# Attention values in four column groups and channel-major projections in a vision tower

## The chip, the cores and the metric

The kernel runs on one core of one Trainium2 chip. All data are float32. The metric is the device time of one launch in microseconds, as the median of the runs shown below. One further execution was taken by the hardware profiler, and all rows below are from it.

## What is computed

64 images of 3 x 224 x 224 pass through a small tower. Each is cut into 196 patches of 16 x 16; a patch becomes a token of 256 channels. Then, with h as the tokens and LN a layer norm without weights:

```python
h  = patches @ W.T + b                                   # tokens, 196 x 256
# selective scan (state space layer), inner width 512, 16 states
xb, z = split(h @ in_proj.T);  xb = silu(causal_conv4(xb))
dt_in, B, C = split(xb @ x_proj.T);  dt = softplus(dt_in * dt_w + dt_b)
state = scan(exp(dt * A) * state + (xb * dt) * B);  y = sum_n(state * C) + xb * D
h  = LN(h + (LN(y) * g + b) * silu(z) @ out_w.T)
# channel mix: token mixed with the token before it
r  = sigmoid(xr @ W_r);  k = square(relu(xk @ W_k));  h = LN(h + r * (k @ W_v))
# attention, 8 heads, queries and keys 4 wide, values 32 wide
s  = leaky_relu(q @ k.T / 2);  h = LN(h + gamma * softmax(s) @ v)
# eight experts, top 2 by the gate
h  = LN(h + sum_e(gate_e * (h @ We_e.T + be_e)))
```

## The kernel before, in words

The program is one software pipeline over images. An image needs 16 groups of scan work (`GROUPS`: four blocks of 128 inner channels times four groups of four states), and the pipeline's time is counted in slots, 16 per image. Each constant `AT_...` is the slot of a step relative to the first scan group of its own image; so at any time the scan of one image lies beside steps of images ahead of it (patches, embedding, convolution at negative slots) and behind it (output, feed-forward, attention, experts at slots up to 90). Every engine has a function `step` that walks through the 16 slots and, within a slot, through its steps in the order in which they are written; engines execute in that order and wait for each other by semaphores. Slots are not synchronised across engines: an engine runs ahead until a semaphore stops it.

**Scan.** In each slot GpSimd (POOL) forms X = u * B for one group (`inputs`, L472, 128 x 784), VectorE (DVE) scans it in two halves (`scan_group`, L1089), POOL multiplies by C (`times_c`, L482), and TensorE (PE) sums the states by transposing matmuls with the identity into YB (`sum_states`, L599). ScalarE (ACT) makes the decay exp(dt * A) into PSUM (`decay`, L892) ahead of each scan half and drains the sums (`drain_y`, L899). X has a ring of six buffers, the decay one of two. u = dt * x is one POOL operation per image (L462).

**PSUM.** Three one-bank tiles G0, G1, G2 and one two-bank tile SB are shared by all other steps. `G0_USES` and its sisters say which steps use which bank, in order of slots; a step waits until the use before it is drained.

**Output.** After the layer norm of y, `turn_y` brings it to channels on partitions, ACT applies gain and bias into y3 (L907), POOL multiplies by silu(z) (L525). `project_out` has tokens on the output's partitions: per block of 98 tokens four products of 256 columns (L620), and the residual hT is added by accumulating transposes (L623).

**Channel mix.** h1 is turned back to channels (`h1T`). r and v are token-major products of 256 columns (`token_major`, L639), k is channel-major (`mix_keys`, L647). ACT drains k with a ReLU (L939), POOL squares it (L515), ACT takes the tanh of r (L934); DVE forms (1 + tanh) * v and adds h1 (L1122, L1125), both token-major.

**Attention.** Queries and keys are two products of 96 output rows each (L656), masked by ACT so that the heads can share a contraction. A unit is four heads of one block of 98 queries; an image has four. Per unit: scores (L668, two row groups of 32 partitions, 392 columns), leaky ReLU (L956), row maximum (DVE, L1136), four exponentials (L963), eight transposes (L678), a PSUM drain (L971), and the values: eight products with the probabilities as the 98 x 98 stationary operand and 33 moving columns (L691), the 33rd being ones, so that the row sum comes out as well. DVE divides and adds the residual (`attended`, L1148 to L1153).

**Loads.** SyncE (SP) issues all DMAs in its own `step` order: pixels in 16 pieces, the projections dt, B, C stored to DRAM and spread back over 128 partitions (L401, L407), the gates likewise (L413, L419), and the output.

`keep_busy` (L546) issues matmuls whose result is used by nobody, at the slots `AT_WARM`, as often as `WARM` says. A float32 matmul of the program appears in the trace as two MATMUL records with their LDWEIGHTS, a transpose as one.

Of the kernel before, what the change touches and what calls it, by code (L numbers as in the profile page):

```python
# [7 lines left out]
ALU = mybir.AluOpType  # L8
# [3 lines left out]
P = 128  # L12
# [6 lines left out]
BLK = 2  # L19
# [22 lines left out]
QKP = 3 * QK  # L42
# [23 lines left out]
AT_TAP = -22  # L66
# [3 lines left out]
AT_XD = -12  # L70
AT_XPROJ = -12
AT_XPROJ_OUT = -12
AT_PROJ_STORE = -12
AT_DT_LOAD = -9
# [10 lines left out]
AT_Y_STATS = 18  # L85
AT_Y_STD = 20
AT_Y_NORM = 21
AT_TURN_Y = 22
AT_YG = 23
AT_Y3 = 25  # L90
AT_OUT = 26
AT_OUT_STATS = 27
# [8 lines left out]
AT_V = 34  # L101
AT_FFN = 35
AT_FFN_STATS = 35
AT_FFN_STD = 38
AT_FFN_NORM = 39
AT_H2T = 41
AT_H2T_OUT = 42
AT_QK = 42
AT_QK_OUT = 43
AT_VALUES = 47  # L110
AT_VALUES_OUT = 48
AT_SCORES = (43, 45, 46, 49,)
# [12 lines left out]
AT_GATE = 68
AT_GATE_IN = 69
AT_GATE_EXP = 70
AT_TOP2 = 70
AT_WS = 70
AT_WS_OUT = 71  # L130
AT_GATE_STORE = 70
AT_GATE_LOAD = 71
AT_H3T2 = 75
AT_SCALE = (75, 75, 76, 77,)
AT_PAIR = (76, 77, 78, 78,)
AT_ACC_OUT = 80
AT_MOE_T = 86
AT_MOE_STATS = 88
AT_MOE_STD = 89
AT_MOE_NORM = 89  # L140
# [54 lines left out]
def vit_tower(nc, x, w_tok, b_tok, w_in, conv_w, conv_b, w_xproj, a_log, d_par, dt_w, dt_b, w_out, ln_g, ln_b,  # L195
              w_r, w_k, w_v, mu_r, mu_k, w_qk, b_q, b_k, w_vv, b_v, gamma, w_g, b_g, w_e, b_e,
              ident, q_mask, k_mask, rank_of, proj, gates, out):
    with ExitStack() as ctx:
# [32 lines left out]
        bk = sb("bk", [QKP, 1])  # L231
        bqm = sb("bqm", [QKP, 2])
        bkm = sb("bkm", [QKP, HU // 2])
# [9 lines left out]
        kmask = sb("kmask", [QKP, HU // 2])  # L243
# [27 lines left out]
        rs = sb("rs", [TB, BLK, D])  # L271
# [6 lines left out]
        vs = [sb(f"vs{i}", [TB, BLK, HEADS, DV + 1]) for i in range(2)]  # L278
# [3 lines left out]
        rg = sb("rg", [TB, HU])  # L282
# [63 lines left out]
        normed = {n: sem(f"normed_{n}") for n in LN}  # L346
        y3_ready = sem("y3_ready")
        before_step = sem("before_step")
# [5 lines left out]
        av_step = sem("av_step")  # L354
        gate_step = sem("gate_step")
# [13 lines left out]
        CONSTS = 16  # L369
# [10 lines left out]
        def _(sp):  # L380
# [40 lines left out]
            def step(b, par):  # L421
                for g in range(GROUPS):
                    def at(slot):
                        return live(b, par, g, slot)

                    for ng in range(GC):
# [4 lines left out]
                    for s, q in at(AT_GATE_STORE):  # L431
                        store_gates(s)
                    for s, q in at(AT_DT_LOAD):
                        after(sp, dt_ready, s)
                        spread_rows(s, dtin[:].rearrange("p (o t) -> p o t", o=1), 0, 1, dtin_landed)
                    for s, q in at(AT_LOAD):
                        load(s)
                    for ng in range(GC):
                        n0 = NG * ng
                        for s, q in at(AT_B[ng]):  # L440
# [925 lines left out]
```

## Time and profile before

| what | us |
|---|---|
| median of 3 runs (lowest to highest) | 4683.52 (4680.42 to 4685.36) |
| the profiled execution's own time | 4687.52 |
| its span | 4685.5 |
| PE busy | 4386.0 (94%) |
| POOL busy | 4332.2 (92%) |
| DVE busy | 3726.6 (80%) |
| ACT busy | 3705.0 (79%) |

The span runs from the first to the last instruction of the profiled execution. Busy is the time in which an engine executed something, over the whole span; the pipeline's fill at the start and its drain at the end are included, so the steady part is denser. Overlapping instructions of one engine are counted once.

### The profile page before, as it was taken

The numbers are of one execution on the slowest core, as the hardware profiler recorded it, in microseconds if no ns is written. First come the engines' busy times: TensorE is split into PE (matmuls) and PEld (weight loads), VectorE is DVE, ScalarE is ACT, GpSimd is POOL, SyncE is SP. The second block draws the span as 40 slices with busy tenths as digits, with TensorE's granted clock in tenths as the row PEclk, the third lists the DMA queues.
The fourth block names the chain that finished last, engine by engine and source line by source line (L and its number), as shares of the span: only waits on it lengthen the run. The fifth ranks groups of instructions, "written<-read, shape, count | busy, mean of one in ns | idle before, by whom it ended". The sixth has DMA issues, their size and how long they took to land.

```text
span 4685.5 us, 92000 instructions
## 1 busy us (share of the span) xinstructions
PE 4386.0 (94%) x31744; PEld 3882.0 (83%) x31744; DVE 3726.6 (80%) x7504; ACT 3705.0 (79%) x8898; POOL 4332.2 (92%) x3272
## 2 busy tenths in 40 slices
PE   4689999999999999999999999999999999999998
PEld 3578888888888888888888888888888888888777
DVE  3578888888888888888888888888888888888753
ACT  4688888888888888888888888888888888888752
POOL 4999999999999999999999999999999999999950
PEclk8799999999999999999999999999999999999987
DMA  4223233223223223223323323323322322322200
GB/s 101 64 68 77 61 76 86 58 71 86 60 74 81 62 76 78 67 70 78 72 67 76 75 64 76 84 58 73 86 59 71 85 61 75 80 65 72 68 18 28
DMA packets 730607, 328.77 MB, mean 70 GB/s; under 512 B 631542, under 2 KB 655392, under 8 KB 729888
## 3 DMA queue, kind: packets, MB, share of 16 engines
q1 hardware_dynamic: 730144, 322.89, 27.9%
q8 instruction: 254, 4.16, 0.4%
q14 instruction: 209, 1.71, 0.1%
HBM read 307.88 MB, written 14.90 MB: 69 GB/s over the span
## 4 chain that ended last, share of the span: by engine, by line
PE 33%; ACT 29%; DVE 23%; issue 7%; POOL 5%; DMA 1%; SPq 1%; ACTq 0%; DVEq 0%; POOLq 0%
PE G L719 15%; DVE X L1089 9%; ACT dA L892 8%; PE YB L599 5%; DVE xbs L1066 4%; PE SB L576 4%; PE SB L668 3%; ACT pT L971 3%; PE G L639 3%; POOL X L482 2%; POOL X L472 2%; ACT y L907 2%; ACT xbs L849 2%; ACT dt L880 2%; ACT ysb L926 2%
## 5 line engine op out<-in xcount | busy, mean ns | idle before, releaser
L1089 DVE TENSOR_TENSOR_SCAN X<-dA,X 128x392 f32<-128x392 f32 x2048 | 1873.3, 957 | 370.2 <-ACT dA L892 327.1
L482 POOL TENSOR_TENSOR X<-X,Cb 128x784 f32<-128x784 f32 x1024 | 1896.9, 1852 | 24.9 <-DVE X L1089 24.6
L472 POOL TENSOR_TENSOR X<-u,Bb 128x784 f32<-128x784 f32 x1024 | 1898.9, 1854 | 7.0 <-DMA Bb<-proj_rows 6.8
L892 ACT ACTIVATE dA<-dt,negA 128x195 f32<-128x195 f32 x4096 | 1519.4, 418 | 144.5 <-DVE X L1089 122.0
L599 PE MATMUL YB<-idn,X 128*98 128x128 f32 x8192 | 1074.5, 276 | 40.1 <-POOL X L482 40.0
L599 PEld LDWEIGHTS YB<-idn,X 128*98 128x98 f32 x8192 | 912.1, 129 | 96.1 <-POOL X L482 50.9
L719 PE MATMUL G<-hg,we 128*128 128x196 f32 x4096 | 723.5, 333 | 7.4 <-DVE hg L1205 7.4
L719 PEld LDWEIGHTS G<-hg,we 128*128 128x128 f32 x4096 | 680.5, 192 | 46.5 <-issue 45.0
L576 PE MATMUL SB<-hT,win 128*128 128x196 f32 x2048 | 373.6, 335 | 34.8 <-ACT hT L840 34.4
L691 PEld LDWEIGHTS G<-vs,pT 98*98 98x98 f32 x4096 | 401.4, 172 | 3.8 <-ACT pT L971 2.4
L691 PE MATMUL G<-vs,pT 98*98 98x33 f32 x4096 | 395.7, 252 | 1.9 <-ACT pT L971 1.9
L576 PEld LDWEIGHTS SB<-hT,win 128*128 128x128 f32 x2048 | 335.3, 190 | 69.8 <-ACT hT L840 50.0
L963 ACT ACTIVATE pr<-pr,nmx 98x196 f32<-98x196 f32 x1024 | 378.3, 450 | 12.9 <-DVE nmx L1136 12.6
L1066 DVE SCALAR_TENSOR_TENSOR xbs<-SB,cw,xbs 128x195 f32<-128x195 f32 (+2 forms) x768 | 267.1, 412 | 94.6 <-ACT xbs L849 90.5
L899 ACT ACTIVATE ysb<-YB 98x256 f32<-98x256 f32 x256 | 97.6, 381 | 250.3 <-PE YB L599 250.3
L956 ACT ACTIVATE pr<-SB 98x784 f32<-98x784 f32 x256 | 209.1, 817 | 93.9 <-PE SB L668 89.9
L567 PE MATMUL G<-patT,wtok 128*128 128x196 f32 x1536 | 272.8, 335 | 1.5 <-ACT patT L831 1.5
L668 PE MATMUL SB<-km,qm 32*98 32x392 f32 x1024 | 233.6, 530 | 36.1 <-DVE xbs L1074 35.1
L567 PEld LDWEIGHTS G<-patT,wtok 128*128 128x128 f32 x1536 | 260.3, 195 | 2.0 <-issue 1.9
L1205 DVE TENSOR_TENSOR hg<-G,Gb 128x784 f32<-128x784 f32 x256 | 241.1, 963 | 21.4 <-PE G L719 18.7
L1136 DVE TENSOR_REDUCE nmx<-pr 98x4 f32<-98x784 f32 x256 | 243.1, 950 | 16.2 <-ACT pr L956 6.6
L620 PE MATMUL G<-wout,y 128*98 128x256 f32 x1024 | 250.9, 389 | 0.0
(145 smaller groups left out, 6621.8 us busy)
## 6 DMA issues: line engine op xcount, KB each, us to landing
Bb<-proj_rows SPq DMA_DIRECT2D x256, 392.0 KB, 4.3
Cb<-proj_rows SPq DMA_DIRECT2D x256, 392.0 KB, 4.9
Gb<-gate_rows SPq DMA_DIRECT2D x64, 784.0 KB, 4.5
px<-in_x SPq DMA_DIRECT2D x1024, 36.8 KB
out<-ob SPq DMA_DIRECT2D x64, 196.0 KB
dtin<-proj_rows SPq DMA_DIRECT2D x64, 98.0 KB, 3.1
we<-in_w_e SPq DMA_DIRECT2D x1, 2048.0 KB
proj_rows<-pj SPq DMA_DIRECT2D x64, 25.3 KB
```

The costliest lines, as they stand in the source:

```text
L472: tt(X[(GROUPS * s + g) % RING][:], u[q % 2][:, c:c + 1, :].broadcast_to([P, NG, T]), Bb[:, NG * ng:NG * (ng + 1), :], ALU.mult).then_inc( ...
L482: tt(t[:], t[:], Cb[:, n0:n0 + NG, :], ALU.mult).then_inc(prod_ready, 1)
L567: last = mm(o[:, m * T:(m + 1) * T], lhsT=wtok[:, k, m * P:(m + 1) * P], rhs=patT[:, half * COLORS + c, :], start=(k == 0), stop=(k == KP ...
L576: last = mm(o[:, j // 2, (j % 2) * T:(j % 2 + 1) * T], lhsT=win[:, k, m * P:(m + 1) * P], rhs=src[:, k, :], start=(k == 0), stop=(k == DC ...
L599: last = mm(YB[0:TB, k * P:(k + 1) * P], lhsT=X[(GROUPS * s + g) % RING][:, j, k * TB:(k + 1) * TB], rhs=idn[:], is_transpose=True, start= ...
L668: last = mm(o[0:TB, j, :], lhsT=qm[mine, n % 2, k * TB:(k + 1) * TB], rhs=km[mine, :, :].rearrange("p h t -> p (h t)"), start=True, stop=True)
L691: last = mm(o[0:TB, j * (DV + 1):(j + 1) * (DV + 1)], lhsT=pT[:, j // 2, at:at + TB], rhs=vs[q % 2][:, k, h0 + j, :], start=(k == 0), stop ...
L719: last = mm(o[:, m * T:(m + 1) * T], lhsT=we[:, k, at:at + P], rhs=hg[p % GRING][:, e, k, :], start=(p == 0 and e == 0 and k == 0 and m == 0),
L892: last = go(dA[i % DRING][:, j, 1:T], dt_[q % 2][:, c, 1:T], ACT.Exp, scale=negA[:, c, n:n + 1])
L963: last = go(pr[i % PRING][:, j, :], pr[i % PRING][:, j, :], ACT.Exp, bias=nmx[i % PRING][:, j:j + 1])
L1066: last = v.scalar_tensor_tensor(out=xbs[:, c, k:], in0=S.tile[:, c // 2, at:at + T - k], scalar=cw[:, c, TAPS - 1 - k:TAPS - k], in1=xbs[: ...
L1089: v.tensor_tensor_scan(t, dA[i % DRING].rearrange("p n t -> p (n t)"), t, 0.0, ALU.mult, ALU.add).then_inc(scan_done, 1)
```

## The change

- The values have the value heads as stationary operand (98 x 32) and the probabilities as moving one (98 columns). The four heads of a unit write to four groups of 32 output partitions, that is four column groups of the array. The result has channels on partitions; ACT copies it out (`drain_values`), PE turns it back (`turn_values`), and DVE's `attended` runs once per block of queries instead of once per unit. The row sums come from the exponentials' `accum_out`.
- Queries and keys come from one product of 128 output rows, 64 for queries and 64 for keys.
- The output projection, r and v are channel-major, with 196 columns. hT is added by DVE (`add_tokens`); the sums are turned to tokens by `turn_back` (`outT`, `ffnT`).
- The gate product moves from POOL to DVE (`gate_y`), the square from POOL to ACT. ACT's gain and bias of y are now applied within PSUM.
- Slots, PSUM bank assignment, and the order of the steps within a slot are new on all engines. The slots of the steps not shown move by a few at most; on POOL the order in a slot becomes: inverse deviation of attention, `inputs`, other inverse deviations, u, and `times_c` last. On SP it becomes: dt's load, pixels, the projections' store, B, the gates' store and spread, the output's store, C.

```diff
-AT_WARM = (2, 5, 14, 17, 11,)
-WARM = (0, 1, 0, 0, 1,)
-AT_LOAD = -34
-AT_PATCH = (-31, -30, -27,)
-AT_PATCH_OUT = (-29, -29, -26,)
+AT_WARM = (10, 10, 11, 8, 8,)
+WARM = (0, 0, 1, 0, 0,)
...
-AT_XPROJ = -12
-AT_XPROJ_OUT = -12
-AT_PROJ_STORE = -12
-AT_DT_LOAD = -9
+AT_XD = -16
+AT_XPROJ = -14
+AT_XPROJ_OUT = -14
+AT_PROJ_STORE = -9
+AT_DT_LOAD = -8
 AT_SOFT = -8
 AT_U = -7
 AT_IN = -1
-AT_TIMES = 2
+AT_TIMES = 1
 AT_DECAY = -1
-AT_B = (-4, -1, 0, 2,)
-AT_C = (1, 3, 2, 4,)
-AT_Y_OUT = (6, 10, 12, 18,)
+AT_B = (-8, -7, -3, -6,)
+AT_C = (-4, -6, 4, 0,)
...
+AT_OUT_ADD = 27
+AT_OUT_T = 28
...
+AT_FFN_T = 37
...
+AT_AV_OUT = (53, 58,)
+AT_TURN_AV = (57, 61,)
...
-G0_USES = {"v": AT_V, "AV2": AT_AV[2], "qk": AT_QK, "h3T2": AT_H3T2, "values": AT_VALUES, "gate": AT_GATE, "h2T": AT_H2T}
-G1_USES = {"moeT": AT_MOE_T, "out": AT_OUT, "h1T": AT_H1T, "patch0": AT_PATCH[0], "r": AT_RK, "AV1": AT_AV[1]}
-G2_USES = {"k": AT_RK, "h3T": AT_H3T, "embed": AT_EMBED, "AV0": AT_AV[0], "patch2": AT_PATCH[2], "xproj": AT_XPROJ, "patch1": AT_PATCH[1], "ws": AT_WS, "AV3": AT_AV[3], "acc": AT_PAIR[0]}
+G0_USES = {"k": AT_RK, "moeT": AT_MOE_T, "qk": AT_QK, "h3T2": AT_H3T2, "values": AT_VALUES, "h3T": AT_H3T, "xproj": AT_XPROJ, "patch1": AT_PATCH[1], "ws": AT_WS, "h2T": AT_H2T}
+G1_USES = {"v": AT_V, "avT0": AT_TURN_AV[0], "gate": AT_GATE, "embed": AT_EMBED, "out": AT_OUT, "outT": AT_OUT_T, "h1T": AT_H1T, "ffnT": AT_FFN_T, "patch0": AT_PATCH[0]}
+G2_USES = {"AV0": AT_AV[0], "patch2": AT_PATCH[2], "r": AT_RK, "AV1": AT_AV[2], "avT1": AT_TURN_AV[1], "acc": AT_PAIR[0]}
...
-                    for s, q in at(AT_KSQ):
-                        pool.wait_ge(where["k"].drained, where["k"].count("k", s))
-                        tt(ka[:], ka[:], ka[:], ALU.mult).then_inc(ksq_ready, 1)
...
-                    for s, q in at(AT_Y3):
-                        pool.wait_ge(S.drained, S.count("turn_y", s))
-                        pool.wait_ge(S.drained, S.count("z", s))
-                        tt(y3[:], y3[:], zs[:], ALU.mult).then_inc(y3_ready, 1)
...
-            def project_out(s, q):
+            def project_out(s):
                 pe.wait_ge(y3_ready, s + 1)
                 o = free("out", s)
+                for m in range(DC):
+                    for c in range(IC):
+                        last = mm(o[:, m * T:(m + 1) * T], lhsT=wout[:, c, m * P:(m + 1) * P], rhs=y3[:, c, :],
+                                  start=(c == 0), stop=(c == IC - 1))
+                last.then_inc(where["out"].filled, 1)
+            def turn_back(s, name, src):
+                o = free(name, s)
                 for k in range(BLK):
-                    tok = slice(k * TB, (k + 1) * TB)
-                    for c in range(IC):
-                        mm(o[0:TB, k * D:(k + 1) * D], lhsT=y3[:, c, tok], rhs=wout[:, c, :],
-                           start=(k == 0 and c == 0), stop=False, skip_group_check=True)
                     for m in range(DC):
-                        last = mm(o[0:TB, k * D + m * P:k * D + (m + 1) * P], lhsT=hT[q][:, m, tok], rhs=idn[:],
-                                  is_transpose=True, start=False, stop=(m == DC - 1), skip_group_check=True)
-                last.then_inc(where["out"].filled, 1)
+                        last = nc.tensor.transpose(o[0:TB, k * D + m * P:k * D + (m + 1) * P],
+                                                   src[:, m, k * TB:(k + 1) * TB], idn[:])
+                last.then_inc(where[name].filled, 1)
...
-            def mix_keys(s):
+            def channel_major(s, name, w, src):
...
-                for i in range(2):
-                    for k in range(DC):
-                        last = mm(o[0:QKP, i * T:(i + 1) * T], lhsT=wqk[:, k, i * QKP:(i + 1) * QKP], rhs=h2T[:, k, :],
-                                  start=(k == 0), stop=(k == DC - 1))
+                for k in range(DC):
+                    last = mm(o[:, 0:T], lhsT=wqk[:, k, :], rhs=h2T[:, k, :], start=(k == 0), stop=(k == DC - 1))
...
-                h0 = HU * (n % 2)
+                i, c = n // (HEADS // HU), n % (HEADS // HU)
                 pe.wait_ge(S.drained, S.count(f"P{n}", s))
                 if n == 0:
                     pe.wait_ge(where["values"].drained, where["values"].count("values", s))
-                o = free(f"AV{n}", s)
-                for j in range(HU):
-                    for k in range(BLK):
+                o = free(f"AV{i}", s) if c == 0 else where[f"AV{i}"].tile
+                for k in range(BLK):
+                    for j in range(HU):
                         at = ((j % 2) * 2 + k) * TB
-                        last = mm(o[0:TB, j * (DV + 1):(j + 1) * (DV + 1)], lhsT=pT[:, j // 2, at:at + TB],
-                                  rhs=vs[q % 2][:, k, h0 + j, :], start=(k == 0), stop=(k == BLK - 1))
-                last.then_inc(where[f"AV{n}"].filled, 1)
+                        last = mm(o[DV * j:DV * (j + 1), c * TB:(c + 1) * TB], lhsT=vs[q % 2][:, k, HU * c + j, :],
+                                  rhs=pT[:, j // 2, at:at + TB], start=(k == 0), stop=(k == BLK - 1),
+                                  skip_group_check=True)
+                last.then_inc(av_half if c == 0 else where[f"AV{i}"].filled, 1)
+            def turn_values(s, i):
+                pe.wait_ge(where[f"AV{i}"].drained, where[f"AV{i}"].count(f"AV{i}", s))
+                o = free(f"avT{i}", s)
+                for c in range(DC):
+                    last = nc.tensor.transpose(o[0:TB, c * P:(c + 1) * P], avT[:, c, :], idn[:])
+                last.then_inc(where[f"avT{i}"].filled, 1)
...
-            def probs(s, n):
+            def probs(s, q, n):
                 act.wait_ge(nmx_ready, UNITS * s + n + 1)
                 i = UNITS * s + n
                 for j in range(HU):
-                    last = go(pr[i % PRING][:, j, :], pr[i % PRING][:, j, :], ACT.Exp, bias=nmx[i % PRING][:, j:j + 1])
+                    h = HU * (n % 2) + j
+                    last = go(pr[i % PRING][:, j, :], pr[i % PRING][:, j, :], ACT.Exp, bias=nmx[i % PRING][:, j:j + 1],
+                              accum_out=esum[q % 2][:, n // 2, h:h + 1])
                 last.then_inc(pr_ready, 1)
             def drain_pT(s, n):
                 o = filled(f"P{n}", s)
                 i = UNITS * s + n
+                if n % 2 == 1:
+                    act.wait_ge(av_half, BLK * s + n // 2 + 1)
+                elif i > 0:
+                    filled(f"AV{(n // 2 - 1) % BLK}", (i - 1) // UNITS)
+                go(pT[:], o[0:TB], ACT.Copy).then_inc(S.drained, 1)
+            def drain_values(s, i):
+                o = filled(f"AV{i}", s)
                 if i > 0:
-                    filled(f"AV{(i - 1) % UNITS}", (i - 1) // UNITS)
-                go(pT[:], o[0:TB], ACT.Copy).then_inc(S.drained, 1)
+                    filled(f"avT{i - 1}", s)
+                elif s > 0:
+                    filled(f"avT{BLK - 1}", s - 1)
+                go(avT[:], o[:, 0:DC * TB].rearrange("p (c t) -> p c t", c=DC), ACT.Copy).then_inc(where[f"AV{i}"].drained, 1)
...
+                        go(ka[:], ka[:], ACT.Square).then_inc(ksq_ready, 1)
...
+            def gate_y(s):
+                dve.wait_ge(y_scaled, s + 1)
+                dve.wait_ge(S.drained, S.count("z", s))
+                if s > 0:
+                    filled("out", s - 1)
+                v.tensor_tensor(y3[:].rearrange("p (a b) t -> p a (b t)", a=2), S.tile,
+                                zs[:].rearrange("p (a b) t -> p a (b t)", a=2), ALU.mult).then_inc(S.drained, 1)
+                dve.wait_ge(S.drained, S.count("turn_y", s))
+                dve.sem_inc(y3_ready, 1)
...
-                v.tensor_tensor(rs[:], rv, h1[:], ALU.add).then_inc(bank.drained, 1)
+                v.tensor_tensor(rs[:], rv, h1T[:, :, 1:], ALU.add).then_inc(bank.drained, 1)
...
-            def attended(s, q, n):
-                k, h0 = n // 2, HU * (n % 2)
-                i = UNITS * s + n
+            def attended(s, q, k):
+                i = BLK * s + k
                 if i > 0:
-                    b = where[f"AV{(i - 1) % UNITS}"]
-                    dve.wait_ge(b.drained, b.count(f"AV{(i - 1) % UNITS}", (i - 1) // UNITS))
-                o = filled(f"AV{n}", s)
-                heads = o[0:TB, 0:HU * (DV + 1)].rearrange("p (h d) -> p h d", h=HU)
+                    b = where[f"avT{(i - 1) % BLK}"]
+                    dve.wait_ge(b.drained, b.count(f"avT{(i - 1) % BLK}", (i - 1) // BLK))
+                o = filled(f"avT{k}", s)
+                heads = o[0:TB, 0:D].rearrange("p (h d) -> p h d", h=HEADS)
                 rows = rg[:].rearrange("p (h o) -> p h o", o=1)
-                mine = slice(h0 * DV, (h0 + HU) * DV)
-                v.reciprocal(rows, heads[:, :, DV:]).then_inc(av_step, 1)
+                v.reciprocal(rg[:], esum[q % 2][:, k, :]).then_inc(av_step, 1)
                 dve.wait_ge(av_step, 2 * i + 1)
-                v.tensor_tensor(heads[:, :, 0:DV], heads[:, :, 0:DV], rows.broadcast_to([TB, HU, DV]),
-                                ALU.mult).then_inc(av_step, 1)
+                v.tensor_tensor(heads, heads, rows.broadcast_to([TB, HEADS, DV]), ALU.mult).then_inc(av_step, 1)
                 dve.wait_ge(av_step, 2 * i + 2)
-                v.scalar_tensor_tensor(out=att[:, k, mine].rearrange("p (h d) -> p h d", h=HU),
-                                       in0=h2[q % 2][:, k, mine].rearrange("p (h d) -> p h d", h=HU), scalar=2.0,
-                                       in1=heads[:, :, 0:DV], op0=ALU.mult,
-                                       op1=ALU.add).then_inc(where[f"AV{n}"].drained, 1)
+                v.scalar_tensor_tensor(out=att[:, k, :], in0=h2[q % 2][:, k, :], scalar=2.0, in1=o[0:TB, 0:D], op0=ALU.mult,
+                                       op1=ALU.add).then_inc(where[f"avT{k}"].drained, 1)
...
+            def add_tokens(s, q):
+                o = filled("out", s)
+                v.tensor_tensor(hT[q][:], o[:, 0:DC * T].rearrange("p (c t) -> p c t", c=DC), hT[q][:],
+                                ALU.add).then_inc(where["out"].drained, 1)
```

## Rows read from the trace of the kernel before

**Rows 1.** Stretch: length; busy us (count) of PE, PEld, DVE, ACT, POOL; clock; DMA.

```profile
585.00:4100.00 3515.00, 3391.16 (x25026) 3012.49 (x25024) 2933.71 (x5899) 2913.26 (x7011) 3416.89 (x2574) 1.00 0.30 73
```

**Rows 2.** Line 462, whole span, then 585 to 4100 us: ns, first and last start.

```profile
L462 POOL TENSOR_TENSOR u<-dt,xbs x64: 1842/1855/1862, 61.9 to 4402.5; 128x784 f32<-128x784 f32 x64
...
L462 POOL TENSOR_TENSOR u<-dt,xbs x50: 1842/1855/1862, 643.0 to 4054.6; 128x784 f32<-128x784 f32 x50
```

**Rows 3.** The page's chain that ended last, by engine.

```profile
PE 33%; ACT 29%; DVE 23%; issue 7%; POOL 5%; DMA 1%; SPq 1%; ACTq 0%; DVEq 0%; POOLq 0%
```

**Rows 4.** Waits, 585 to 4100 us: total us, times, longest.

```profile
POOL ka L515 <- ACT ka L939: 45.6, 51, 0.9
POOL X L482 <- DVE X L1089: 20.4, 51, 0.7
...
ACT ysb L899 <- PE YB L599: 206.1, 51, 4.0
ACT SB L860 <- DVE xbs L1066: 134.8, 51, 2.9
```

**Rows 5.** Groups by line and form, 1000 to 3880 us: busy, mean ns, idle before.

```profile
L525 POOL TENSOR_TENSOR y<-y,zs 128x784 f32<-128x784 f32 x41 | 75.7, 1846 | 0.0
...
L515 POOL TENSOR_TENSOR ka<-ka 128x392 f32<-128x392 f32 x41 | 34.5, 841 | 36.7 <-ACT ka L939 36.7
```

**Rows 6.** Timeline of PE: start, duration, operation, records merged.

```profile
2040.81 1.49 PE L656 MATMUL G<-h2T,wqk 128*96 128x196 f32 x8
2042.14 1.50 PE L691 MATMUL G<-vs,pT 98*98 98x33 f32 x16
2043.47 1.95 PE L620 MATMUL G<-wout,y 128*98 128x256 f32 x8
2045.25 0.38 PE L623 MATMUL G<-idn,hT 128*98 128x128 f32 x2
2045.47 1.89 PE L620 MATMUL G<-wout,y 128*98 128x256 f32 x8
...
2058.88 0.90 PE L668 MATMUL SB<-km,qm 32*98 32x392 f32 x4
2059.71 0.55 PE L631 MATMUL G<-idn,h 98*128 98x98 f32 x4
...
2071.10 1.89 PE L639 MATMUL G<-wr,xr 128*98 128x256 f32 x8
2072.82 1.49 PE L647 MATMUL G<-xk,wk 128*128 128x196 f32 x8
2074.15 0.84 PE L678 MATMUL SB<-idn,pr 98*98 98x98 f32 x8
2074.82 1.04 PE L599 MATMUL YB<-idn,X 128*98 128x128 f32 x8
```

**Rows 7.** The view of rows 5, on DVE and ACT.

```profile
L1205 DVE TENSOR_TENSOR hg<-G,Gb 128x784 f32<-128x784 f32 x168 | 158.2, 963 | 0.0
...
L1150 DVE TENSOR_TENSOR G<-G,rg 98x128 f32<-98x128 f32 x165 | 49.4, 300 | 6.0 <-DVE rg L1148 0.4
...
L840 ACT ACTIVATE hT<-G,btok 128x196 f32<-128x196 f32 x82 | 29.4, 408 | 0.0
...
L939 ACT ACTIVATE ka<-G 128x392 f32<-128x392 f32 x41 | 19.8, 483 | 0.0
...
L1003 ACT ACTIVATE G<-G 98x16 f32<-98x16 f32 x41 | 6.9, 168 | 0.0
```

**Rows 8.** Timeline of SP: two issues one behind the other.

```profile
2097.89 0.29 SPq L413 DMA_DIRECT2D gate_rows<-wsT  x1
...
2099.16 0.34 SPq L419 DMA_DIRECT2D Gb<-gate_rows  x1
```

**Rows 9.** The page's DMA issues: count, KB, median us to landing.

```profile
dtin<-proj_rows SPq DMA_DIRECT2D x64, 98.0 KB, 3.1
```

**Rows 10.** The view of rows 1, in the tail.

```profile
4530.00:4560.00 30.00, 28.16 (x145) 24.31 (x146) 12.42 (x31) 8.70 (x21) 4.81 (x9) 0.74 0.10 35
```

More of the change, by code:

```diff
@@ L277, in vit_tower @@
         km = sb("km", [QKP, HU // 2, T])
-        vs = [sb(f"vs{i}", [TB, BLK, HEADS, DV + 1]) for i in range(2)]
+        vs = [sb(f"vs{i}", [TB, BLK, HEADS, DV]) for i in range(2)]
         pr = [sb(f"pr{i}", [TB, HU, T]) for i in range(PRING)]
@@ L281, in vit_tower @@
         nmx = [sb(f"nmx{i}", [TB, HU]) for i in range(PRING)]
-        rg = sb("rg", [TB, HU])
+        rg = sb("rg", [TB, HEADS])
+        esum = [sb(f"esum{i}", [TB, BLK, HEADS]) for i in range(2)]
+        avT = sb("avT", [P, DC, TB])
         att = sb("att", [TB, BLK, D])
@@ L499, in at @@
                         return live(b, par, g, slot)
-                    for k in range(GROUPS):
-                        for s, q in at(k + AT_TIMES):
-                            times_c(s, k)
                     for s, q in at(AT_ATT_STD):
@@ L730, in turn_moe @@
                 pe.wait_ge(accT_ready, s + 1)
-                o = free("moeT", s)
-                for k in range(BLK):
-                    for m in range(DC):
-                        last = nc.tensor.transpose(o[0:TB, k * D + m * P:k * D + (m + 1) * P],
-                                                   accT[:, m, k * TB:(k + 1) * TB], idn[:])
-                last.then_inc(where["moeT"].filled, 1)
+                turn_back(s, "moeT", accT)
             def step(b, par):
@@ new lines, in step @@
+                    for i in range(BLK):
+                        for s, q in at(AT_TURN_AV[i]):
+                            turn_values(s, i)
+                    for n in range(UNITS):
+                        for s, q in at(AT_TURN_P[n]):
+                            turn_probs(s, n)
+                    for s, q in at(AT_XPROJ):
+                        xproj(s)
+                    for s, q in at(AT_WARM[0]):
+                        keep_busy(WARM[0])
+                    for part in range(3):
+                        for s, q in at(AT_PATCH[part]):
+                            patches(s, part)
@@ new lines, in step @@
+                    for s, q in at(AT_GATE):
+                        gate(s, q)
+                    for n in range(UNITS):
+                        for s, q in at(AT_SCORES[n]):
+                            scores(s, n)
+                    for s, q in at(AT_MOE_T):
+                        turn_moe(s)
+                    for p in range(PAIRS):
+                        for s, q in at(AT_PAIR[p]):
+                            expert_pair(s, p)
+                    for s, q in at(AT_TURN_Y):
+                        turn_y(s)
@@ new lines, in step @@
+                    for s, q in at(AT_XB):
+                        pe.wait_ge(where["embed"].drained, where["embed"].count("embed", s))
+                        project_in(s, hT[q], "xb", 0)
+                    for s, q in at(AT_WARM[3]):
+                        keep_busy(WARM[3])
+                    for s, q in at(AT_WARM[1]):
+                        keep_busy(WARM[1])
+                    for s, q in at(AT_H3T2):
+                        turn(s, "h3T2", h3)
+                    for s, q in at(AT_VALUES):
+                        token_major(s, "values", h2T, wvv)
@@ L836, in drain_embed @@
                 if s >= CYCLE:
-                    filled("out", s - CYCLE)
+                    filled("outT", s - CYCLE)
                 o = filled("embed", s)
```

455 lines of the change are left out of this document (223 added, 232 removed).

## The prediction

> **What bounds the kernel now.** The table of engines by stretch comes first [rows 1]. Over 3515 us of steady work PE is busy 3391.16, POOL 3416.89, DVE 2933.71 and ACT 2913.26. An image's period is read from an operation that occurs once per image, u = dt·x on POOL [rows 2]: 643.0 to 4054.6 us is 49 periods, 69.62 us each; 4402.5 is five more. The nine before 643.0 took (643.0 − 61.9)/9 = 64.6 each, because the late stages had no images yet. So of an image's 69.62 us POOL works 67.68 (3416.89/3515 × 69.62), PE 67.17, DVE 58.11, ACT 57.70. Two engines are full within 3%, and the other two have 11.5 and 11.9 us idle.
>
> The chain of waits [rows 3] gives POOL 5% and PE, ACT and DVE 85% together. I read that as a net of short handovers, not as POOL being free: with POOL idle 1.94 us per image, nothing can gain more than 1.94 unless POOL is relieved. The waits [rows 4] say what those 1.94 are: 45.6/51 = 0.89 for ka (POOL waits for the ReLU behind a late PE), 20.4/51 = 0.40 for a scan, and 0.65 of gaps between instructions. Conversely PE has 2.45 idle, so relieving POOL alone would give little more. The change relieves both.
>
> **POOL.** It loses the gate product (1.846) and the square (0.841) [rows 5]: 67.68 − 2.69 = 64.99. The ka wait goes with the square. With the 0.65 of gaps the floor is 65.64; what is late next is the scan behind which C's product waits. That product now comes one slot earlier (`AT_TIMES` 2 to 1) but last in the slot instead of first; X was filled nearly two slots (some 8 us) before, so a scan may come a few us late at no cost. Bounds for POOL's new waits: 0 and today's 1.29.
>
> **PE** [rows 6]. Pitches are differences of starts. A record of 196 columns takes 1.33/8 = 0.166, one of 256 takes 1.72/8 = 0.215 to 1.78/8 = 0.222, a 128-column transpose 0.22/2 = 0.11, a 98-column one 0.67/8 = 0.084.
> - Output projection: 2 × (1.78 + 0.22) = 4.00 before; after, 16 × 0.166 = 2.66 and four transposes of hT, 0.44: −0.90.
> - r and v: 1.72 to 1.33 each, −0.78; `ffnT` adds four transposes, +0.44.
> - Queries and keys: 8 records become 4, −0.66.
> - Filler matmuls: two calls become one, 2 × 0.166, −0.33.
> - `avT`: 2 × 2 transposes, +0.44.
> - Values: four units of 16 records, 1.33 each (5.32 in all), bound by the 98 weight columns. After: 16 records of 98 columns per unit, 0.084 each if nothing overlaps, 1.34: no gain. With four column groups in full overlap, 1.34/4 = 0.34: −4.0. A cost above today's is possible as well: the loads have 32 columns rather than 98, but the groups alternate, and if each load stood ahead of its matmul at half a pitch more, the units would cost 2.0 each, +2.7. The nearest row is the scores' two row groups: 4 records of 392 columns took 0.83, against 4 × 0.33 = 1.33 one after the other, a factor of 0.62. I take 0.60 per unit, since four groups should do somewhat better than two: 2.4, −2.9.
>
> The Trainium skill has two rules here, neither of which enters the sum. TensorEngine Tiling (Array Packing), under Tiling Modes, says that changing the tiling mode drains the engine: this speaks against the change, which enters and leaves a new mode four times per image; a drain of one 98-column record each way would be 8 × 0.084 = 0.7 (an estimate), and PE's saving 3.9 instead of 4.7. TensorE: Matmul & The Clock Gate, under Why this matters for your kernels, has three 32-wide column tiles at 2.38× for 512 columns; by it the units would take about 1.34/2.38 = 0.56 (an estimate). The scores' factor of 1.6 with two groups agrees in kind; no row shows column groups.
>
> Sum: −0.90 − 0.78 + 0.44 − 0.66 − 0.33 + 0.44 − 2.9 = −4.7, PE 62.5 (61.4 to 68.1 with the bounds). Even with no gain from the groups PE would be at 65.4, level with POOL.
>
> **ACT** [rows 7]. Square of 128x392, as the ReLU: +0.48. Two drains of 128x196 from PSUM, 0.408 each: +0.82. tanh of r on 392 instead of 512 columns: −0.1. The rest is reordered, not added. New is the row sum out of each of the 16 exponentials. The trace has no such output. Bounds: nothing, or a whole further activation, 16 × 0.408 = 6.5. The nearest row is the smallest activation, 98x16, 0.168: I take it, 2.7. ACT: 57.7 + 3.9 = 61.6 (58.9 to 65.4).
>
> **DVE** [rows 7]. The gate product, 128x784: +0.96. The residual add, half as wide: +0.48. Values: four units, each a small operation and two of 128 columns at 0.300, become two, each a small one and two of 256 columns; these cost between one and two times 0.300, I take 0.45: 4 × 0.60 − 2 × 0.90 = −0.6, and two small ones less (0.168 for a small one on ACT), −0.3. The two feed-forward operations on 392 columns instead of 512: −0.3. Together +0.2 (0 to +1), DVE 58.3.
>
> **SP and the order.** Storing the projections moves from slot −12 to −9 and dt's load to −8, the slot of its softplus. Both now stand behind the store of the gates and their spreading. That spread was issued 1.27 us after the store [rows 8], so the chain is gates' store, 1.3 to the spread, 0.4 to the projections' store, 1.3 to dt's load, 3.1 to its landing [rows 9]: 6.1 us from the draining of ws (slot 5) to dt (slot 8), which are over two slots of 4.2 apart. I cost it at nothing; two slots of other work hide it. If ws came a slot late, ACT would wait up to 2 us and POOL's u behind it, since u now stands ahead of C's product. B and C loads wait for POOL as before; each is issued a slot or more before its use against a landing time of under 5 us.
>
> **The sum.** POOL 64.99 + 0.65 + waits. ACT now has 4 us of slack instead of 11.9 and DVE 7.3, so handovers have less room; but PE, which caused the waits shown, has 3.2 and more. I take 0.9 of waits: a period of 66.5, 3.1 less. There are 54 steady periods: 167. The nine early ones have the two removed operations in most images and POOL busy throughout: 9 × 1.5 = 14. The tail after the last scan is PE's (28.16 of 30 us busy at a granted clock of 0.74 [rows 10]); three images still have their values ahead, 3 × 2.9/0.74 = 12, less the transposes in the last image's chain: 9. Total 190. The profiled execution took 4687.52 around a span of 4685.5, 4.0 above the median of 4683.52: 4687.5 − 190 = 4497, and less 4, 4493; I say **4490**.
>
> **Rivals.**
> - *POOL's floor.* Period 65.7, as the ka wait was most of what POOL had. 54 × 3.9 + 14 + 12 = 237: 4447. For: POOL waited for nothing else steady but 0.40. Against: ACT and DVE are both denser. 13%.
> - *Handovers hold part of it.* ACT waited 206.1/51 = 4.0 for the state sums and 134.8/51 = 2.6 for the convolution [rows 4]. If ACT's 61.6 keeps these 6.6, the period is 68.2: 54 × 1.4 + 14 + 9 = 99, 4585. Against: the first wait was slack, PE behind POOL. 20%.
> - *dt's load is late* in most images, 1.5 us: 68.0, about 4595. 4%.
> - *Slower: ACT is the bound.* If the row sum costs as much as an activation, 0.408, ACT has 65.4, and with 6.6 of waits 72.0: 54 × 2.4 = 130 slower, less 20, 4795. It decides where ACT's work and waits pass 69.6: at 0.26 per row sum with these waits. For: POOL, DVE and PE all stand behind ACT's in-order queue. 7%.
> - *Slower: TensorE's clock.* It was 1.00 in all steady stretches [rows 1] and 0.74 in the tail, where the other engines are light. If, with PE relieved to 94% and filler removed, it were 0.9 on average (between the two levels, 1.2 and 2.4 GHz), PE would need 62.5/0.9 + 2.45 = 71.9, 4800; it decides below 0.93. Against: the work then stretches and closes the gaps. 4%.
> - *The groups don't overlap*: PE 65.4 + 2.45 = 67.9, about 4585 (within the second rival's range). 6%.
>
> The forecast itself has 44%, with 4450 to 4540 as its own range; 2% are left for no change. Less than 0.2% (9.4 us) can't be told from no change. Faster: 44 + 13 + 20 + 4 + 6 = 87%; same 2%; slower 11%. The range leaves out the slower cases and the last of the floor: 4425 to 4640.
>
> **What would show it.** POOL's busy share in the steady stretch stays at 97 to 98%, and u's starts lie 66.5 apart. The 16 value records of a unit span about 0.6 us to the next group's start (1.34: no overlap). Between exponentials of a group either nothing or an extra ACT instruction shows; ACT's busy share is 92 to 93%, DVE's 88%, PE's 94%, clock 1.00. POOL's wait for ka is gone and none above 0.5 us per image has come. Wrong would be: a period over 68, POOL waiting over 2 us per image on DVE or ACT, or a clock below 1.

## The result and the profile after

| | before | after |
|---|---|---|
| median, us | 4684.44 (4680.42 to 4689.01, 4 runs) | 4511.91 (4511.26 to 4513.82, 4 runs) |
| profiled execution: own time, span | 4687.52, 4685.5 | 4511.59, 4509.8 |

The median before is over one execution more than in the table ahead of the prediction. The ratio is 0.9632, with a 95% interval of 0.9615 to 0.9649: 3.7% faster. Forecast was 4490 within 4425 to 4640.

The first view of after is the busy time by stretch, to be read against [rows 1] (a stretch of 3315 us, since the kernel ends earlier), and then u's row against [rows 2].

```profile
585.00:3900.00 3315.00, 3131.39 (x24670) 2732.26 (x24668) 2906.11 (x5597) 2947.36 (x7839) 3223.74 (x2424) 1.00 0.31 75
```

```profile
L471 POOL TENSOR_TENSOR u<-dt,xbs x64: 1835/1850/1881, 60.9 to 4244.0; 128x784 f32<-128x784 f32 x64
...
L471 POOL TENSOR_TENSOR u<-dt,xbs x49: 1841/1849/1881, 627.4 to 3842.0; 128x784 f32<-128x784 f32 x49
```

The period is (3842.0 − 627.4)/48 = 66.97 us, against 69.62. Of it POOL works 65.13 (3223.74/3315), PE 63.26, ACT 59.54, DVE 58.71. The spans' difference of 175.7 splits as follows: 54 steady periods, 3759.5 before (643.0 to 4402.5) and 3616.6 after (627.4 to 4244.0), 142.9; nine early ones 14.6; the stretch from the last u to the end, 283.0 to 265.8, 17.2; the first u starts 1.0 earlier.

The chain that ended last, to be read against [rows 3], has left PE (33% to 4%) for DVE and ACT (52% to 81% together):

```profile
DVE 41%; ACT 40%; issue 8%; POOL 5%; PE 4%; SPq 1%; DVEq 0%; DMA 0%; ACTq 0%; POOLq 0%
```

The waits of after, 585 to 3900 us, against [rows 4]. POOL's wait for ka is gone; two others have come, 1.16 us per image together (39.2/50 = 0.78 and 18.5/49 = 0.38). ACT's great wait is no longer for the state sums but for the scores.

```profile
POOL X L481 <- PE YB L601: 39.2, 50, 0.8
POOL veps_out L496 <- DVE mv_out L1146: 18.5, 49, 0.7
...
ACT pr L972 <- PE SB L672: 203.3, 147, 2.1
ACT dA L908 <- DVE X L1137: 121.5, 148, 1.1
...
DVE X L1137 <- ACT dA L908: 116.6, 156, 1.1
DVE ob L1151 <- POOL rstd_moe L500: 91.6, 49, 2.2
```

PE's timeline of after has the new form of the values beside its neighbours, against [rows 6]. 16 records take 2009.92 − 2009.44 = 0.48 us to the next start, where 1.33 were. Queries and keys take 2038.11 − 2037.28 = 0.83, the output projection 2.65.

```profile
2009.44 0.55 PE L695 MATMUL G<-pT,vs 98*32 98x98 f32 x16
2009.92 0.42 PE L596 MATMUL YB<-idn,xD 128*98 128x128 f32 x2
...
2037.28 0.90 PE L661 MATMUL G<-h2T,wqk 128*128 128x196 f32 x4 [0.30 <-ACT h2T L927]
2038.11 0.55 PE L695 MATMUL G<-pT,vs 98*32 98x98 f32 x16
...
2039.51 2.82 PE L621 MATMUL G<-y,wout 128*128 128x196 f32 x16
2042.16 0.38 PE L596 MATMUL YB<-idn,xD 128*98 128x128 f32 x2
```

ACT's timeline of after shows the row sums as instructions of their own. Each row lasts 0.19 to 0.23 us, but overlaps its neighbours: exponentials start 2002.21 − 2001.77 = 0.44 apart, 0.35 of which is the exponential, so a read adds 0.09.

```profile
2001.77 0.44 ACT L980 ACTIVATE pr<-pr,nmx 98x196 f32<-98x196 f32 x1
2002.12 0.19 ACT L980 ACTIVATION_READ_ACCUMULATOR pr<-pr,nmx 98x1 f32 x1
2002.21 0.44 ACT L980 ACTIVATE pr<-pr,nmx 98x196 f32<-98x196 f32 x1
```

### The profile page after: what moved, and what is told of

It reads as the page before. It is cut to its first block, busy times and chain, and to the rows that moved or that the text cites. A ratio compares the mean times of both kernels' runs of the same rounds, so it can differ in the third digit from the quotient of the medians.

```text
span 4509.8 us, 93215 instructions
## 1 busy us (share of the span) xinstructions
PE 4113.7 (91%) x31872; PEld 3579.4 (79%) x31872; DVE 3763.7 (83%) x7246; ACT 3819.7 (85%) x10114; POOL 4168.0 (92%) x3144
## 4 chain that ended last, share of the span: by engine, by line
DVE 41%; ACT 40%; issue 8%; POOL 5%; PE 4%; SPq 1%; DVEq 0%; DMA 0%; ACTq 0%; POOLq 0%
DVE X L1137 19%; ACT dA L908 12%; ACT pr L980 6%; DVE xbs L1103 4%; DVE hg L1248 4%; ACT pT L991 3%; POOL X L491 2%; ACT xbs L865 2%; DVE nmx L1184 2%; POOL X L481 2%; ACT dt L896 2%; ACT ysb L940 2%; ACT L908 2%; ACT L896 2%; ACT xD L883 1%
## 5 line engine op out<-in xcount | busy, mean ns | idle before, releaser
L731 PE MATMUL G<-hg,we 128*128 128x196 f32 x4096 | 705.1, 333 | 4.1 <-DVE hg L1248 4.1
L980 ACT ACTIVATE pr<-pr,nmx 98x196 f32<-98x196 f32 x1024 | 456.0, 456 | 1.8 <-DVE nmx L1184 1.8
L682 PE MATMUL SB<-idn,pr 98*98 98x98 f32 x2048 | 218.5, 250 | 34.7 <-DVE zs L1116 30.9
L682 PEld LDWEIGHTS SB<-idn,pr 98*98 98x98 f32 x2048 | 188.1, 128 | 50.0 <-issue 49.5
L637 PEld LDWEIGHTS G<-idn,h 98*128 98x128 f32 x1024 | 101.8, 143 | 146.3 <-DVE h L1151 69.2
L991 ACT ACTIVATE pT<-SB 98x784 f32<-98x784 f32 x256 | 206.7, 808 | 3.9 <-PE SB L682 3.9
```

The costliest lines, as they stand in the source:

```text
L682: last = nc.tensor.transpose(o[0:TB, j // 2, at:at + TB], pr[(UNITS * s + n) % PRING][:, j, k * TB:(k + 1) * TB], idn[:TB, :TB])
L731: last = mm(o[:, m * T:(m + 1) * T], lhsT=we[:, k, at:at + P], rhs=hg[p % GRING][:, e, k, :], start=(p == 0 and e == 0 and k == 0 and m == 0),
L980: last = go(pr[i % PRING][:, j, :], pr[i % PRING][:, j, :], ACT.Exp, bias=nmx[i % PRING][:, j:j + 1], accum_out=esum[q % 2][:, n // 2, h:h ...
```

## The experiments

All medians are of four or more runs; ratios are to the kernel before in the same series.

**Relief in the old plan.** Three kernels made from the kernel before, their slots and order unchanged except for the moved steps.

```diff
 # before_pool_relief (ACT, DVE; the two POOL steps are gone)
+ go(ka[:], ka[:], ACT.Square).then_inc(ksq_ready, 1)
+ v.tensor_tensor(y3[:], y3[:], zs[:], ALU.mult).then_inc(y3_ready, 1)
 # before_pe_relief: queries and keys in one product, and
-WARM = (0, 1, 0, 0, 1,)
+WARM = (0, 0, 0, 0, 0,)
 # before_both_relief: both
```

> The kernel before, with only the square moved to ACT and the gate product moved to DVE; the plan is the old one. POOL loses 2.69 us of 67.68 per image. Theory A (two full engines, PE and POOL): the gain is capped by PE, which had 2.45 us idle of 69.62 per image and needs some of it for its handovers; period 68.3 to 69.3, 20 to 80 us less: 4605 to 4665. Theory B (POOL alone is the bound): the whole 2.69 and the wait for the ReLU come back, period 66.0, about 4470. Theory C (the net of handovers through ACT and DVE bounds, POOL is off the path): 4680 or more, as ACT and DVE become denser.

> The kernel before, with only queries and keys in one product and without the two filler calls: PE loses 8 records of 196 columns, about 1.3 us of 67.17 per image; POOL keeps its 67.68. Theory A (two full engines): only POOL's wait for the ReLU (0.89 per image) and its 0.40 for a scan can shrink; period 68.7 to 69.5, 10 to 55 us less: 4630 to 4675. Theory B (POOL alone): at most the 0.89, about 4630. Theory C (PE alone): 1.3 per image, 4600.

> The kernel before with both: square and gate product off POOL, queries and keys in one product, no filler. Theory A (two full engines): the two gains add to more than their sum, since each alone is capped by the other engine; period about 67.5, 4550. Theory B (POOL alone): as with POOL's relief alone. If it is slower than 4600, the old plan, and not the amount of work, holds the period, and the new plan is worth the rest of the 173 us.

Measured: 5018.68 (ratio 1.0713, 1.0697 to 1.0729), 4746.11 (1.0131, 1.0114 to 1.0148), 5077.31 (1.0843, 1.0827 to 1.0859). All are slower, the second by less than 2%. The first agrees in sign with its theory C and the third with the theory that the old plan holds the period, neither of which had said how much; the second is outside all three. The groups by form (busy, mean ns) and then the timeline of POOL in before_pool_relief show one reason:

```profile
L1082 DVE TENSOR_TENSOR y<-y,zs 128x784 f32<-128x784 f32 x38 | 222.6, 5857 | 0.0
```

```profile
2039.00 1.85 POOL L482 TENSOR_TENSOR X<-X,Cb 128x784 f32<-128x784 f32 x1 [3.56 <-DVE X L1090]
2040.81 1.86 POOL L472 TENSOR_TENSOR X<-u,Bb 128x784 f32<-128x784 f32 x1
2046.45 0.20 POOL L487 TENSOR_TENSOR veps_out<-mv_out,epsc 98x2 f32<-98x2 f32 x1 [3.78 <-DVE mv_out L1099]
```

DVE's product of two SBUF operands takes 5.86 us beside a streaming POOL, not 0.96; the scans behind it come late, and POOL, which it was to relieve, waits. The second is the clock, which follows from such waits where PE stops for them. The steady stretches of the two single reliefs, where [rows 1] have 1.00:

```profile
585.00:4100.00 3515.00, 3249.66 (x23190) 2865.18 (x23189) 2979.69 (x5523) 2717.04 (x6551) 3050.95 (x2290) 0.97 0.28 67
```

```profile
585.00:4100.00 3515.00, 3329.19 (x24215) 2959.31 (x24214) 2893.44 (x5806) 2863.08 (x6896) 3359.16 (x2532) 0.98 0.29 71
```

In before_pe_relief, stretches of 4 us and PE's timeline show where TensorE goes to its lower level (1.2 of 2.4 GHz): PE was busy 2.46 of 4 us at the full clock, with a stop of 1.54 us ahead of the scores, and the next stretch has 0.61.

```profile
2076.00:2080.00 4.00, 2.46 (x24) 2.23 (x24) 3.86 (x11) 2.21 (x5) 3.92 (x4) 1.00 0.66 137
2080.00:2084.00 4.00, 4.00 (x15) 3.40 (x14) 3.86 (x7) 2.37 (x5) 4.00 (x4) 0.61 0.74 70
```

```profile
2079.80 0.90 PE L666 MATMUL SB<-km,qm 32*98 32x392 f32 x4 [1.54 <-DVE xbs L1073]
```

Read from the trace to more digits, the lower level holds for 122.9 of the 3515 us, which is 61 us of full-rate PE time lost; 62 is the measured loss. In before_pool_relief it holds for 211.6 us; half of that is 106 of the 335 lost.

**The two causes apart.** The old plan again: y scaled within PSUM, so that DVE's product reads SBUF only once (its slot is also 23 instead of 25, where the change has it, so that two things differ from before_pool_relief); and the merged product with the filler kept.

```diff
 # before_relief_psum
+ go(mine, mine, ACT.Identity, scale=lng[:, c:c + 1], bias=lnb[:, c:c + 1])   # within PSUM
+ v.tensor_tensor(y3_wide, S.tile, zs_wide, ALU.mult).then_inc(S.drained, 1)
 # before_qk_filler: before_pe_relief with
 WARM = (0, 1, 0, 0, 1,)
```

> POOL's relief in the old plan again, but with y scaled within PSUM and the gate product of DVE reading one operand from PSUM, as the change has it. In before_pool_relief that product, with both operands in SBUF, took a median of 5881 ns (975 to 11009) beside a busy POOL. Theory A (the operand's place made the difference): the product takes 0.97 us, DVE is back under 60 us per image, and the time is 4590 to 4690, at least 330 us below 5019. Theory B (the old plan has no place for the product on DVE, whatever it costs): it stays above 4850.

> The kernel before with queries and keys in one product, the filler calls kept: PE has 0.66 us less per image. before_pe_relief, which also dropped the filler, showed stretches at the lower clock in its steady part (mean 0.98) and took 62 us more. Theory A (the clock fell because PE had become idle where the filler was): here the clock is 1.00 in the steady part and the time is 4650 to 4685. Theory B (the shorter product itself opens the gap): the clock falls as well, 4720 to 4750.

Measured: 4747.98 (1.0136, 1.0119 to 1.0152) and 4683.47 (0.9999, 0.9989 to 1.0009). The product takes 0.95 again:

```profile
L1083 DVE TENSOR_TENSOR y<-SB,zs 128x784 f32<-128x784 f32 x64 | 60.7, 948 | 0.8 <-ACT SB L900 0.7
```

That is 271 us of the 335 that before_pool_relief had lost; the product's own time is the placement's, what the earlier slot gave isn't separated. Theory A had asked for 330 and at most 4690, theory B for more than 4850: both missed, and it stays 64 us slower than the kernel before. Its POOL waits 169.6/50 = 3.4 us per image for the output norm's moments, all that it was relieved of and more, and the clock is 0.99 (the lower level holds for 85.3 us, 43 us lost).

```profile
POOL veps_out L488 <- DVE mv_out L1103: 169.6, 50, 5.6
POOL X L483 <- DVE X L1094: 74.7, 101, 1.1
```

The merged product with the filler kept has a clock of 1.00 and gains nothing. With the product merged, the 62 us hang on the filler; the filler taken out of the unmerged product was not run. A filler call now stands ahead of the same scores, and the stop there is 1.21 us instead of 1.54:

```profile
2046.27 0.49 PE L546 MATMUL YB<-win,idn 128*98 128x196 f32 x2
2049.19 0.90 PE L666 MATMUL SB<-km,qm 32*98 32x392 f32 x4 [1.21 <-DVE xbs L1073]
```

**The same questions in the new plan.**

```diff
 # after_no_filler
-WARM = (0, 0, 1, 0, 0,)
+WARM = (0, 0, 0, 0, 0,)
 # after_gate_sbuf: ACT writes y3 in SBUF, and DVE
+ v.tensor_tensor(y3[:], y3[:], zs[:], ALU.mult).then_inc(y3_ready, 1)
 # after_gate_pool: the same on POOL, behind the inverse deviation of y
+ tt(y3[:], y3[:], zs[:], ALU.mult).then_inc(y3_ready, 1)
```

> The changed kernel without its one filler call per image (0.33 us of PE). Theory A (the filler holds the clock): stretches at the lower clock appear in the steady part, one or so per image, and it takes 20 to 120 us more than 4512. Theory B (PE is dense enough without it, and PE isn't the bound): 4512 within 10 us.

> The changed kernel with y scaled into SBUF, so that DVE's gate product has both operands there. Theory A (DVE can't get at SBUF for such a product while POOL works): it takes several us instead of 0.97, the scans behind it come late, and the kernel takes 4750 to 4950, more than the kernel before. Theory B (an accident of the old plan): 0.97 us, 4512 within 15.

> The changed kernel with only the gate product back on POOL (and y scaled into SBUF for it): POOL gets 1.81 us per image more, DVE 0.97 less. Theory A (in the new plan POOL bounds, with waits of 1.17 that can absorb little): 54 x 1.8 and the early images, 100 to 120 us more, 4610 to 4630. Theory B (in the new plan the handovers of DVE and ACT bound, 81% of its chain of waits): 0 to 50 more, as POOL's waits shrink instead.

Measured: 4514.88, 4559.84 and 4597.36 (0.9817, 0.9802 to 0.9831), against 4511.91. The filler does nothing any more (theory B). The gate product from SBUF costs 48, between the two theories. Its row (min/median/max ns, then first and last start) is mostly normal, with a worst case of ten times. What is held instead is a short instruction of POOL, 194/942/1016 where after has 194/195/196. Both rows, and then one case from the timelines of DVE and POOL:

```profile
L1126 DVE TENSOR_TENSOR y<-y,zs x64: 940/942/9866, 158.4 to 4404.3; 128x784 f32<-128x784 f32 x64
L503 POOL TENSOR_TENSOR shift_ffn<-shift_ffn,rstd_ffn x64: 194/942/1016, 233.4 to 4450.8; 98x2 f32<-98x2 f32 x64
...
2052.61 0.94 DVE L1126 TENSOR_TENSOR y<-y,zs 128x784 f32<-128x784 f32 x1
2052.66 0.94 POOL L503 TENSOR_TENSOR shift_ffn<-shift_ffn,rstd_ffn 98x2 f32<-98x2 f32 x1
```

VectorE starts first here, and POOL's instruction ends with VectorE's product (2053.60 and 2053.55). This makes 52 of POOL's 64 such instructions about 0.75 us longer, but the period only 0.2 (a median of 67.1 against 66.9). Where POOL's train of products starts first, VectorE is held, as in the old plan: five steady products last 4.3 to 4.5 us, and the two periods around each are together 3.2 to 4.9 us longer. Nine early periods take 14 us more (580.6 against 566.5), 54 steady ones at 67.48 instead of 66.97 take 28. One of the five, DVE and then POOL:

```profile
1848.37 4.33 DVE L1126 TENSOR_TENSOR y<-y,zs 128x784 f32<-128x784 f32 x1
...
1850.03 1.85 POOL L481 TENSOR_TENSOR X<-u,Bb 128x784 f32<-128x784 f32 x1
1851.84 0.93 POOL L496 TENSOR_TENSOR veps_moe<-mv_moe,epsc 98x2 f32<-98x2 f32 x1
```

With the product on POOL the time rises by 85, below theory A's range and above B's, the period to (3847.3 − 639.3)/47 = 68.26, and the chain is POOL's:

```profile
POOL 81%; issue 7%; PE 6%; ACT 3%; DVE 2%; SPq 1%; DMA 0%; POOLq 0%; DVEq 0%; ACTq 0%
```

So 1.3 of the product's 1.81 us show. POOL bounds there; without the product its own cycle would be 68.26 − 1.81 = 66.45, which is close to the 66.97 of after, not quite.

**What holds 66.97.** Row sums left out; X buffers added; POOL's step for the last norm earlier.

```diff
 # after_ring8
-RING = 6
+RING = 8
 # after_moe_first_ring8: the same, and on POOL
+for s, q in at(AT_MOE_STD): inverse_std(s, "moe")      # ahead of inputs(), was behind
 # after_no_rowsum: no accum_out; esum is set to 1 once
```

> The changed kernel with eight X buffers instead of six. In its trace POOL waits 39.2/50 = 0.8 us per image for PE to free an X buffer and 0.4 for the moments of the output norm. Theory A (POOL is the bound and its waits are what is left): the first wait goes, 54 x 0.8 = 40 us less, 4470. Theory B (the chain over DVE's scans and ACT's decays bounds): POOL then waits elsewhere, less than 10 us of change, 4505.

> The changed kernel with eight X buffers and, in POOL's slot, the inverse deviation of the last norm ahead of the X product instead of behind it. after_ring8 moved POOL's wait for PE (0.8 us per image) to a wait for the output norm's moments (62.7/49 = 1.3), that is for DVE, which itself stood 48.3/49 = 1.0 for POOL's inverse deviation of the last norm. Theory A (the ring of waits POOL to DVE to POOL holds the period): with both taken away POOL's waits fall to under 0.4, period 66.0 to 66.3, 4460 to 4480. Theory B (DVE's stall was slack as well; scores and the convolution hold DVE): the wait turns up at another of DVE's operations and the time stays at 4505 to 4517.

> The changed kernel with the row sums left out: the exponentials have no accumulator output, and the divisor is a constant. The trace has 16 reads of the accumulator per image, 0.20 us each by their rows, but 0.09 by the distance of the next exponential: ACT has 1.4 us per image less. Theory A (ACT is not on the path, POOL bounds): 4505 to 4512. Theory B (the chain over DVE and ACT bounds, and I underpriced this): 54 x 1.4 = 75 less, 4437.

Measured: 4515.20, 4513.83 and 4503.04. The first two are theory B; the third gains 9 us, 2 more than theory A's range and far from theory B's 75. The first two removed the waits that they aimed at, and the waits came back one step on. POOL in after_ring8, and POOL and DVE in after_moe_first_ring8:

```profile
POOL veps_out L496 <- DVE mv_out L1146: 62.7, 49, 1.6
```

```profile
POOL veps_out L496 <- DVE mv_out L1146: 61.4, 49, 1.6
...
DVE rg L1194 <- PE G L704: 124.8, 49, 2.6
```

POOL's 0.8 + 0.4 became 1.3 for DVE. DVE had waited 1.9 for POOL's inverse deviation and 0.7 for PE's turned values (32.3/49); with the first removed, the second is 2.5, and the sum is what it was. Without row sums the period is (3836.7 − 626.8)/48 = 66.87, and the chain has moved to PE. I read this as PE's cycle being only 0.1 us shorter than the one over DVE and ACT; no run lengthened PE's work to test it:

```profile
PE 47%; DVE 21%; ACT 20%; POOL 6%; issue 4%; SPq 1%; DMA 0%; DVEq 0%; ACTq 0%; POOLq 0%
```

**How the groups overlap.**

```diff
-for k in range(BLK):
-    for j in range(HU):
+for j in range(HU):
+    for k in range(BLK):
```

> The changed kernel with the loops of the values swapped: both blocks of one head, then the next head, so that four records in a row go to one column group instead of two. In the changed kernel 16 records take 0.48 us to the next operation's start (0.030 each, against 0.084 for one of 98 columns alone). Theory A (records start in order, and one waits for the record before it in its own group): overlap remains only where the group changes, a unit takes 0.8 to 1.2, PE 1.3 to 2.9 us more per image; after_no_rowsum's chain has PE at 47% with a period only 0.1 shorter, so PE is near to bounding: 4550 to 4640. Theory B (each group queues by itself): 0.48 as before and 4512 within 8.

Measured: 4514.63. The unit takes 2011.44 − 2010.95 = 0.49 instead of 0.48: four records in a row to one group cost next to nothing. Theory B.

```profile
2010.95 0.57 PE L695 MATMUL G<-pT,vs 98*32 98x98 f32 x16
2011.44 0.42 PE L596 MATMUL YB<-idn,xD 128*98 128x128 f32 x2
```

No run puts the old form of the values back into the new plan, so what the column groups themselves are worth in time was not measured. An estimate: PE's 63.26 with the 3.4 us per image back (below) would be 66.7 of a period of 66.97, and its seven stops would no longer fit.

## Why the prediction was right, and where it was not

- **POOL's work.** 64.99 forecast, 65.13 measured. The ka wait went, as said. Waits 0.9 forecast, 1.16 measured, and gaps 0.68 (65.13 + 1.16 + 0.68). The period of 66.5 became 66.97: 54 × 0.47 = 25 us more than forecast. The tail gave 8 of them back by an error the other way, so that the sum came out nearer (190 forecast, 175.7 measured on the spans) than its main term.
- **What is late next.** This step was wrong in kind. The scan behind C's product holds POOL no longer; the X buffer (0.78 us) and the output norm's moments (0.38) do, and the first is above the 0.5 that was named as a limit. I had taken POOL for the bound, with removable waits on top, and gave 13% to its floor. Two experiments that took such waits away gained nothing, and the chain has DVE and ACT at 81%. I read the period as a near tie of several cycles: DVE with ACT at 66.97, PE at no more than 66.87, POOL about 66.45 with its wait for the X buffer. That the time landed in the forecast's range owes something to this tie: a forecast from POOL's work alone comes out close.
- **"The change relieves both", and neither alone.** The claim that POOL's relief alone gives little more held in sign only: in the old plan it lost 64 us, and PE's alone gave 0. The two together, with the product from SBUF and no filler, lost 393 us; with the product from PSUM and the filler they were not run. What the runs show is that the work taken off POOL counts in the new plan (85 us for the product alone) and not in the old one; how much of the 173 us is the plan's, the column groups' or the channel-major products' can't be split further by them. (Two small slips in my working: PE's idle 2.45 of 69.62 is 3.5%, not within 3%; and 4.7 less 0.7 is 4.0, not 3.9.)
- **The product on DVE** at 0.96 was right (L1126 took a median of 969 ns), but by luck: the price was from L1205, which reads PSUM, and my working did not name that as a condition. The same product from SBUF cost 48 us in the new plan and turned the old one's relief into a loss of 335.
- **PE.** 62.5 forecast, 63.26 measured: −3.9 instead of −4.7. Summed over the starts of all records of the steady images, the forecast's own terms come to −4.6: values −3.41 (a unit took 0.48; forecast 0.60, bounds 0.34 and 2.0), the output projection with its transposes −0.68 instead of −0.90, r and v −0.84, queries and keys −0.50 instead of −0.66, `avT` +0.71 instead of +0.44, `ffnT` and filler as forecast. The misses cancel in this sum. The term that was left out is +0.7 in operations that the change doesn't touch: the last record ahead of a values unit takes 0.09 longer, and a first record after a stop takes longer too (0.24 instead of 0.17 at 2037.28), with seven stops for other engines per image instead of four. For queries and keys both show: four records take 0.83 in after, and 2039.90 − 2039.23 = 0.67 in before_qk_filler, behind no stop and ahead of the old values:

```profile
2039.23 0.83 PE L655 MATMUL G<-h2T,wqk 128*128 128x196 f32 x4
2039.90 1.50 PE L689 MATMUL G<-vs,pT 98*98 98x33 f32 x16
```

- **ACT.** 61.6 forecast, 59.54 measured. The row sum was mis-sized: 0.168 each by the smallest row, 0.09 by pitch, 1.2 us less per image. The drains of the values took 0.324 each by their rows and 0.21 by pitch, not 0.408, 0.4 less for the two. Leaving the sums out gained 9 us, so ACT's amount of work did not bound and that rival was far off. Its busy share was 89%, not 92 to 93%.
- **DVE.** 58.3 forecast, 58.71 measured.
- **The clock** stayed at 1.00 in the steady part. The rival was real elsewhere: with the filler gone from the old plan and the product merged it cost 62 us, at a mean of 0.98.
- **Early images and tail.** 14 forecast, 14.6 measured; tail 9 forecast, 17.2 measured: the last image's own scans, one period, also became 2.7 shorter and I had not counted them. The other 5.5 stay open.

## What to carry over

Before moving an elementwise product from GpSimd to VectorE, look at where its operands lie, and take its price from a row with the same placement. In a pipeline with four engines above 80%, time a relief together with its new order: alone it can lose, and a wait that is removed tends to reappear at the next handover. Filler matmuls are worth a run without them, in each plan anew.

## What the runs showed of the hardware

- A VectorE `tensor_tensor` of 128x784 with both operands in SBUF took a median of 5881 ns (975 to 11009) while GpSimd streamed its own products, and a mean of 948 with one operand in PSUM (before_relief_psum). In the timeline of before_pool_relief one runs from 2030.42 to 2036.27. GpSimd began new products at 2031.80 and 2033.60 and stood idle only from 2035.44 to 2039.00; 0.83 us after it stopped, VectorE was through. By these rows VectorE got nothing in while GpSimd's products followed one another. The Trainium skill has the mechanism (SBUF — State Buffer, Who interferes with whom): a VectorE instruction with two SBUF inputs contends with a GpSimd instruction that reads SBUF, and the second to issue blocks. The runs agree in both directions: in after_gate_sbuf, with VectorE first, GpSimd's short instruction took 942 ns instead of 195. But VectorE's wait was for a train of instructions, not for one. What ends it is open: in before_pool_relief GpSimd stood idle, while at 1851.84 in after_gate_sbuf VectorE came in ahead of a short instruction that was issued directly behind the train and was itself held (0.93 us).

```profile
L1082 DVE TENSOR_TENSOR y<-y,zs x64: 975/5881/11009, 163.9 to 4864.9; 128x784 f32<-128x784 f32 x64
```

- Four column groups ran 16 float32 records of 98 columns in 0.48 us, 0.030 each, against 0.084 for such a record alone, in either order of the loops (0.49 in the other). Read record by record, the record ahead of a unit takes 0.09 us longer to the next start than its equals (0.26 instead of 0.17 for 196 columns; the fourth unit stands behind a stop and can't be read so), and the last record of each unit takes 0.18, where the last of a round of four inside the unit takes 0.06 to 0.09. That is about 0.1 each way, some 0.7 us per image. The scores' two row groups show the same on entry in before (0.20 instead of 0.11 behind the state sums). The Trainium skill states that a change of tiling mode drains the engine (TensorEngine Tiling (Array Packing), Key Properties). The rows agree, and the prediction's estimate of 0.7 for it, left out of the sum, was close.
- An accumulator read on ScalarE is an instruction of its own, 0.20 us by its row and 0.09 by pitch.
